# Two-stage transformer kernel on one core: mask rows sent two tiles earlier, a V copy and a table load moved at the turn of a row, and the next layer's weights loaded in the last row of a layer

## The reference, cut to what matters

```python
# first stage, per batch: 16 heads of 8, 256 queries, 1601 keys
scores = einsum('bhqd,bhkd->bhqk', qh, kh) / sqrt(8); scores = where(mask, -1e9, scores)
x1 = x + tanh(g_xattn) * (softmax(scores) @ vh @ w_o + b_o)
# second stage, six layers: 16 heads of 64, windows of 32 tokens and the window before
qkv = shift_tokens(x) @ Wqkv;  q, k = l2norm(q) * qs, l2norm(k) * ksc;  rotary(q), rotary(k)
x = x + softmax(8 * q k^T + local_mask) v @ Wo
xn = layernorm(shift_tokens(x)) ;  a, gate = split(xn @ W1 + b1)
x = x + (a * gelu(gate)) @ W2 + b2
out = x1 + tanh(g_ffn) * x
```

## Time and profile before

| | us |
|---|---|
| median of 3 runs (lowest, highest) | 5991.94 (5977.54, 5996.71) |
| the profiled execution: time, span | 6002.82, 6001.0 |
| PE busy | 5562.2 (93%) |
| ACT busy | 4052.7 (68%) |
| DVE busy | 3590.1 (60%) |
| POOL busy | 2654.8 (44%) |
| PE matmuls / POOL instructions | 51848 / 2280 |

### The profile page before, as it was taken

The page is one execution under the profiler, slowest core; times in us unless marked ns, Lnnn a source line. Parts: engine busy times, 40 slices in busy tenths (PEclk is TensorE's granted clock), DMA queues, the critical chain, the costliest instruction groups (busy, mean ns, idle before and its releaser), DMA issues.

```text
span 6001.0 us, 161497 instructions
## 1 busy us (share of the span) xinstructions
PE 5562.2 (93%) x51848; PEld 3310.2 (55%) x51848; DVE 3590.1 (60%) x7913; ACT 4052.7 (68%) x10886; POOL 2654.8 (44%) x2280
## 2 busy tenths in 40 slices
PE   5999999999999879999999999999998999999997
PEld 2444444444444356666666666666665666656665
DVE  3666666666666546655666566656665566556654
ACT  2555554555545467887878777877787778877885
POOL 2111221112211055655555555655565555655563
PEclk9999999999999989999999999999999999999998
DMA  3333233333334043233323333333333323333332
GB/s 79 68 73 62 56 69 64 74 59 58 67 65 74 14 134 98 89 95 108 100 92 92 102 104 94 92 96 108 94 92 97 106 94 92 93 111 93 92 93 74
DMA packets 146300, 512.29 MB, mean 85 GB/s; under 512 B 31996, under 2 KB 48252, under 8 KB 127404
## 3 DMA queue, kind: packets, MB, share of 16 engines
q1 hardware_dynamic: 144300, 506.02, 32.2%
q10 hardware_dynamic: 1536, 0.40, 0.0%
HBM read 223.41 MB, written 30.68 MB: 42 GB/s over the span
## 4 chain that ended last, share of the span: by engine, by line
PE 47%; ACT 9%; issue 4%; DVE 2%; DMA 1%; ACTq 0%; SPq 0%; POOL 0%; DVEq 0%; POOLq 0%
PE b_qk L1420 9%; PE b_c L1461 6%; PE b_o L1382 6%; PE b_pt L1363 5%; PE b_sc L1351 4%; PE b_nv L1398 3%; PE b_qk L1431 3%; PE b_nv L1451 2%; ACT probs L1131 2%; PE b_sc L1342 2%; PE b_c L1491 2%; ACT L78 1%; PE b_nv L1491 1%; ACT L1170 1%; DMA v<-v 1%
## 5 line engine op out<-in xcount | busy, mean ns | idle before, releaser
L441 ACT ACTIVATE eT<-b_e 128x512 f32<-128x512 f32 (+1 forms) x1664 | 907.6, 594 | 972.1 <-PE b_e L759 966.5
L1131 ACT ACTIVATE probs<-b_sc,nb,rq 128x96 f32<-128x96 f32 (+1 forms) x3072 | 1322.4, 449 | 41.1 <-DVE nb L1265 41.1
L514 DVE CUSTOM_DVE_ANT_0 junk<-b_s,mq 128x1024 bf16<-128x1024 f32 (+1 forms) x1024 | 1000.3, 991 | 436.8 <-PE b_s L741 412.2
L1062 POOL TENSOR_TENSOR probs<-probs,rsums 128x512 f32<-128x512 f32 (+1 forms) x768 | 716.4, 933 | 752.1 <-DVE rsums L1201 745.3
L1256 DVE TENSOR_REDUCE b_sc<-b_sc 128x4 f32<-128x512 f32 (+1 forms) x768 | 486.3, 633 | 878.0 <-PE b_sc L1351 877.7
L1121 ACT ACTIVATE probsT<-b_pt 128x512 f32<-128x512 f32 x768 | 457.5, 596 | 601.0 <-PE b_pt L1363 596.7
L1420 PE MATMUL b_qk<-xs,weights 128*128 128x256 f32 x3072 | 751.3, 389 | 87.7 <-POOL xs L1054 49.1
L755 PE MATMUL b_e<-mk,identb 128*128 128x512 bf16 (+1 forms) x1664 | 656.2, 394 | 54.2 <-DMA q_op<-mp 44.2
L1382 PEld LDWEIGHTS b_o<-probsT,v 128*64 128x64 f32 x9216 | 376.8, 138 | 572.6 <-issue 502.2
L1420 PEld LDWEIGHTS b_qk<-xs,weights 128*128 128x128 f32 x3072 | 562.8, 193 | 177.0 <-issue 64.5
L759 PE MATMUL b_e<-q_op,k_op 75*128 75x256 bf16 (+1 forms) x3328 | 659.3, 280 | 0.0
(11 more groups left out here) (132 smaller groups left out, 8344.9 us busy)
## 6 DMA issues: line engine op xcount, KB each, us to landing
rot_p<-rot_s SPq DMA_DIRECT2D x768, 256.0 KB, 2.4
rkb<-rk_scr SPq DMA_DIRECT2D x192, 512.0 KB, 5.9
k_op<-k_scr SPq DMA_DIRECT2D x576, 100.1 KB
v<-v SPq DMA_DIRECT2D x192, 256.0 KB, 3.6
k_scr<-kp SPq DMA_DIRECT2D x48, 400.2 KB, 3.5
ctxT<-in_ctx SPq DMA_DIRECT2D x17, 800.5 KB, 20.2
weights<-in_ffn_w SPq DMA_DIRECT2D x24, 512.0 KB, 5.3
q_op<-q_scr SPq DMA_DIRECT2D x144, 64.0 KB
```

Source lines behind the costliest of these rows:

```text
L441: nc.scalar.activation(eT[0:n, g % 2, i * 512:(i + 1) * 512], b_e[i][0:n, :], ACT.Exp).then_inc(s["e_ready"], 1)
L514: nc.vector.tensor_tensor_reduce(junk[:, half, 0:n], b_s[u % 2][:, 0:n], mq[:, p, qt, half * 1024:half * 1024 + n], 1.0, LOWEST, ALU.add, ...
L1062: nc.gpsimd.tensor_tensor(pu, pu, rsums[:, u % 2, :].unsqueeze(2).to_broadcast([P, 4, w]), ALU.mult).then_inc(s["pn_ready"], 1)
L1131: last = nc.scalar.activation(probs[:, t, k % 2, 2 * e + h, c0:P], b_sc[:, 512 * e + h * w:512 * e + (h + 1) * w], ACT.Exp, bias=nb[:, k % ...
```

## The change

It has three parts.

1. First stage: `TURN` is 5 instead of 7, and the three DMAs of the mask rows stand at tile `TURN + 3` = 8 instead of 10. The K projections move to tiles 3, 4, 6 and 7, the split of K on ACT by one tile (8 and 11), and POOL makes the mask rows of group 0 ahead of the first subtraction for K instead of behind it.
2. Second stage, turn of a row: the copy of the fourth V piece goes from ACT to DVE, behind the gate copies, with a semaphore of its own (`v3_kept`), and the exp and ln tables are loaded behind the first `probsT` of the next iteration instead of ahead of it.
3. Second stage, layers: the last two iterations of a layer stand outside the inner loop (five trips are left), and in the last one SP loads the next layer's scales, K, Q and V weights as soon as the last product that reads each has run; POOL makes the next layer's tables in its step 7. After layer 6 a further, unused set of weights (zeros) is loaded.

```diff
-TURN = 7
+TURN = 5
...
-                at += [(0, 3, "k", 0), (0, 4, "k", 1), (0, 5, "k", 2), (0, 6, "k", 3), (0, 9, "mean_q", 0),
-                       (0, 11, "var_q", 0), (1, 1, "q", 0), (1, 3, "v", 0), (1, 5, "v", 1), (1, 9, "v", 2),
+                at += [(0, 3, "k", 0), (0, 4, "k", 1), (0, 6, "k", 2), (0, 7, "k", 3), (0, 9, "mean_q", 0),
+                       (0, 11, "var_q", 0), (1, 1, "q", 0), (1, 3, "v", 0), (1, 7, "v", 1), (1, 9, "v", 2),
...
-                        if nxt and at == (0, 7):
+                        if nxt and at == (0, 8):
...
-                        if nxt and at == (0, 10):
+                        if nxt and at == (0, 11):
...
-                        if kt == 10:
+                        if kt == TURN + 3:
...
-                with hinted_loop(nc, eng, 1, NB // 2 - 1) as i:
+                with hinted_loop(nc, eng, 1, NB // 2 - 2) as i:
...
+                b = NB - 4
+                iteration(row(layer, b + 2, 0), row(layer, b + 1, 1), row(layer, b, 0), row(layer, b - 1, 1))
+                iteration(row(layer, b + 3, 1), row(layer, b + 2, 0), row(layer, b + 1, 1), row(layer, b, 0), LAST)
...
-                if not isinstance(layer, int):
-                    last = layer * NB - 1
-                    wait_apart(sp, sp_passed, s["qk_done"], count("qk_done", last, 8))
-                    load_scales(layer)
-                    load(PART_K, layer)
-                    load(PART_Q, layer)
-                    wait_apart(sp, sp_passed, s["v_done"], count("v_done", last, 4))
-                    load(PART_V, layer)
...
+                        if i == 1 and begin == LAST:
+                            load_scales(layer + 1)
+                            wait_apart(sp, sp_passed, s["qk_done"], count("qk_done", n, 4))
+                            load(PART_K, layer + 1)
...
+                    if begin == LAST:
+                        wait_apart(sp, sp_passed, s["qk_done"], count("qk_done", n, 8))
+                        load(PART_Q, layer + 1)
...
+                    if begin == LAST:
+                        wait_apart(sp, sp_passed, s["v_done"], count("v_done", n, 4))
+                        load(PART_V, layer + 1)
...
+                    if begin == LAST and k == 7:
+                        pool.wait_ge(scales_in, 16 * here[0] + 32)
+                        wait_apart(pool, pool_passed, s["rotc_ready"], count("rotc_ready", A[0], 8))
+                        scale_tables()
...
+                    if D and k == 0:
+
+                        load_tables(nc, act, EXP_LN_TABLES)
...
-                    if A and k >= 4:
+                    if A and 4 <= k < 7:
...
-                    load_tables(nc, act, EXP_LN_TABLES)
...
+                    if A and k == 7:
+                        n, _, p, _ = A
+                        dve.wait_ge(s["v_done"], count("v_done", n, 4))
+
+                        dve.wait_ge(s["o_done"], count("o_done", n, UNITS, back=2))
+                        nc.vector.tensor_copy(v[:, p, 1, 512:1024], b_qk[:, 512:1024]).then_inc(s["v3_kept"], 1)
```

More of the change, by code:

```diff
@@ L44 @@
 AHEAD = 2
+LAST = 3
 HX, DK = 16, 8
@@ L374, in iteration @@
                 for q in range(4):
[L375 to L379, removed]
                     if nxt and q == 1:
@@ L390, in iteration @@
                         max_parts(row, q)
+                    if nxt and q == 0:
+                        b = nxt[0]
+                        pool.wait_ge(s["khi_ready"], count("khi_ready", b, 1))
+                        nc.gpsimd.tensor_tensor(kf[:, :], kf[:, :], kp[:, 0, :], ALU.subtract
+                                                ).then_inc(s["kres_ready"], 1)
                     if nxt and q == 0:
@@ L829, in ffn_phase @@
                    norm_done=2, ln_ready=2, rn_ready=2, rnk_ready=1, rk_out=32, rkb_in=32, rqt_done=1, rq_ready=2,
-                   sum_ready=4, kn_ready=2, v_done=4, v_kept=4, vmid_in=32,
+                   sum_ready=4, kn_ready=2, v_done=4, v_kept=3, v3_kept=1, vmid_in=32,
                    scores_done=8, max_ready=8, nb_ready=8, exp_ready=8, rsum_ready=8, pn_ready=8,
@@ L837, in ffn_phase @@
                      rk_out="sp", rkb_in="sp", vmid_in="sp", rqt_done="pe", rq_ready="dve", sum_ready="pool", kn_ready="pool",
-                     v_done="pe", v_kept="act", scores_done="pe", max_ready="dve", nb_ready="dve", exp_ready="act",
+                     v_done="pe", v_kept="act", v3_kept="dve", scores_done="pe", max_ready="dve", nb_ready="dve", exp_ready="act",
                      rsum_ready="dve", pn_ready="pool", pt_done="pe", pt_kept="act", o_done="pe",
@@ L988, in iteration @@
                     n, _, p, _ = A
-                    wait_apart(sp, sp_passed, s["v_kept"], count("v_kept", n, 4))
+                    wait_apart(sp, sp_passed, s["v_kept"], count("v_kept", n, 3))
+                    wait_apart(sp, sp_passed, s["v3_kept"], count("v3_kept", n, 1))
                     wait_apart(sp, sp_passed, s["o_done"], count("o_done", n, UNITS, back=2))
@@ L1000, in _ @@
             sp.dma_start(out, xT[:, :, :]).then_inc(out_sent, 16)
+            sp.wait_ge(scales_in, 16 * DEPTH + 16)
+            for part in (PART_K, PART_Q, PART_V):
+                sp.wait_ge(part_in[part], 16 * DEPTH + 16)
             sp.wait_ge(out_sent, 16)
@@ L1015, in _, with scale_tables @@
             pool.wait_ge(consts_in, 16 * N_CONSTS)
+            here = [None]
             def layer_start(layer):
-                pool.wait_ge(scales_in, 16 * layer + 16)
-                wait_apart(pool, pool_passed, s["rotc_ready"], count("rotc_ready", layer * NB, 0))
+                here[0] = layer
+                if isinstance(layer, int):
+                    pool.wait_ge(scales_in, 16)
+                    scale_tables()
+            def scale_tables():
                 for i, col in enumerate((P_Q, P_Q, P_K, P_K)):
@@ L1368, in values @@
                     t, j0 = u // 4, 2 * (u % 4)
-                    pe.wait_ge(s["v_kept"], count("v_kept", n, 4))
+                    pe.wait_ge(s["v_kept"], count("v_kept", n, 3))
+                    pe.wait_ge(s["v3_kept"], count("v3_kept", n, 1))
                     if t == 1:
@@ L1414, in iteration @@
                             if i < 2:
-                                pe.wait_ge(s["v_kept"], count("v_kept", n, 3 + i, back=1))
+                                if i == 0:
+                                    pe.wait_ge(s["v_kept"], count("v_kept", n, 3, back=1))
+                                else:
+                                    pe.wait_ge(s["v3_kept"], count("v3_kept", n, 1, back=1))
                             else:
@@ L1634 @@
                           L0_xattn_b_k, L0_xattn_w_v, L0_xattn_b_v, L0_xattn_w_o, L0_xattn_b_o)
[L1635 to L1636 removed]
+    arrays.update(ffn_w=one_more(layer_weights(L0_ffn_Wqkv, L0_ffn_Wo, L0_ffn_W1, L0_ffn_W2)),
+                  ffn_vec=one_more(layer_vectors(L0_ffn_q_scale, L0_ffn_k_scale, L0_ffn_ln_g, L0_ffn_ln_b, L0_ffn_b1,
+                                                 L0_ffn_b2)),
                   rot=rotary_tables(), lmask=local_constants(),
```

3 lines of the change are left out of this document (1 added, 2 removed).

## The result

The changed kernel takes 5919.1 us (median of 4 runs, 5908.2 to 5932.1), the kernel before 5993.8 (4 runs) on the same chip: the ratio is 0.9883, with an interval of 0.9868 to 0.9899. It is 75 us faster by the medians and 70 by the ratio; 160 were forecast, and the time lies above the range. The profiled execution has a span of 5930.3 against 6001.0.

The account below looks back on a forecast made before the run. It took PE's work, its standstills and a lowered clock as the bound. Savings of 50 (first stage), 92 (turn of a row) and 18 (layers), 160 us, took the median 5991.9 to 5832; range 5770 to 5895.

Parts of the forecast that it names:

- First stage: -50 forecast: First stage: shorter mask-row waits and less half clock, minus a new `q_op` wait, save 50 us, between 0 and 95.
- the last of that part: First stage: moved K projections, POOL order and ACT split of K add no instruction and were costed at nothing.
- the mask rows' wait: First stage, PE before the transposed scores: of 44.2 us, 22 go at q = 3 and about 10 at q = 2.
- The new wait for `q_op`: First stage, near tile 5 of q = 2: PE waits 1 us a batch for `q_op`, 15 us in all.
- The granted clock: First stage: PE's granted clock was to rise from 0.96 to 0.98.
- the price of half clock: First stage: each us at half clock was priced at 0.47 us lost, some 66 us in the stage.
- the very term of the forecast: First stage: half of the 66 us lost to half clock goes with the waits, 33 us saved.
- Turn of a row: -92 forecast: Second stage: PE no longer waits before `b_o`; each of 92 rows gains 1.0 us, bounds 30 to 135 in all.
- Both limits: Second stage, turn of a row: `hT` and the exponentials limit the gain to 1.0 us, not the wait's 1.47.
- Layers: -18 forecast: Second stage, layer tops: four gain 3 us each, the first 7, layer 6's last row loses 1; between 0 and 40.
- The straight-line iterations cost nothing: Second stage: iterations moved outside the inner loop cost 0, as rows 39.07 us apart, some already straight, showed no stall.
- the first stage gives nothing: Rival, chance 0.20: the first-stage standstill moves from tile 0 to tile 5 of q = 2; 5882 us, up to 5905.

Follow-up runs that it names:

- kres_small: Changed kernel with POOL's first-stage subtraction for K cut to 16 columns, the rest of the residue left out; ratio 0.9821 to the kernel before.
- cross_only: Kernel before with only the first-stage part of the change; ratio 1.0047 to the kernel before, 28 us slower.
- q_first: Changed kernel with SP's stores of Q and `q_op` loads put ahead of the `k_op` loads of group 0; ratio 0.9923 to the kernel before.
- best: Changed kernel with DVE's `mneg` before reciprocals, `y` after tile 9's maxima, POOL's `mq` after q = 1's maxima, no inner layer loop; ratio 0.9744 to the kernel before.
- mq_late: Changed kernel with POOL's product `mq` moved behind the maxima of q = 1, a group later; ratio 0.9843 to the kernel before.
- turn_only: Kernel before with only the V copy on DVE and the later table load; ratio 0.9853 to the kernel before, 88 us faster.
- copy_only: Kernel before with only the V copy moved to DVE, the second table load staying ahead of `probsT`; ratio 0.9909 to the kernel before, 55 us faster.
- layers_only: Kernel before with only the shortened inner loop and the early weight loads and tables; ratio 1.0006 to the kernel before.
- ffn_only: Changed kernel with its first-stage part taken back; ratio 0.9856 to the kernel before.
- straight: Changed kernel without the inner loop of a layer, all sixteen iterations straight code; ratio 0.9897 to the kernel before.
- turn6: Changed kernel with TURN 6 instead of 5 and K projections at tiles 3, 4, 5 and 7; ratio 0.9910 to the kernel before.

## Why the prediction was right and wrong

**First stage: -50 forecast, +24 in the trace (+16 and +28 by the ratios).** The step that failed is the last of that part: "The moved K projections, the POOL order and the ACT split of K add no instruction; PE shows no standstill at them and the K chain is used a group later, so I cost them at nothing." They do add no instruction. But they put POOL's subtraction and `mq` later, onto `y` and `xq`, and with `TURN` at 5 they put a K projection behind `mneg`, with a reciprocal of 1.74 us and a product of 0.65 ahead of it on DVE. That was 24.2 us (the fall of the `smax` wait in `kres_small`), 16.4 and 19.0, some 60 us of PE's time that my sum had at nothing. Taken away one by one they gave 30, 25 and 27 us, clock and all; taken away together the stage is 44 us shorter than before, near the 50.

The other terms of this part held. Of the mask rows' wait the forecast had all 22 us ahead of q = 3 go, and 10 of those ahead of q = 2: by group it fell from 19.9 to 2.9 and from 24.3 to 15.3. In `cross_only` it fell to 2.6 and, for q = 2, not at all (25.7). Ahead of q = 2 the DMAs stayed behind the `k_op` loads, which `q_first` showed. The new wait for `q_op` came at the place named, 13.0 us by the list where I had 15. Some of that is luck: the 10.1 us by which I placed it are those of the store `q_scr<-qp`, and the landing of the loads that PE waits for stands in no row.

The granted clock rose from 0.96 to 0.97, not 0.98. Why it rose isn't shown: PE waited 98.5 us in the five rows above, where it was 52.3 before, and with the same first stage `cross_only` has 0.96. By the price of half clock 0.01 is worth 16 us here, so more waits and the better clock make 46 - 16 = 30 us, near the 24. `best` has the term whole: its four waits are 58.3 us in all (8.8 of it one wait in the last batch), about the 52.3 of the kernel before, and yet the stage is 44 us shorter; by the price (0.47, from one stretch of one batch) its 0.98 in place of 0.96 is worth 0.02 x 2 x 1745 x 0.47 = 33 us, the very term of the forecast, as far as a clock printed to two places can tell. That the clock falls less there because the waits are short ones is argued, not shown.

That `y` and `xq` are slow because of POOL's instructions beside them is shown twice, from both sides: `kres_small` freed one, `mq_late` the other. The Trainium skill, "SBUF — State Buffer", section "SBUF: two separate sides", has the rule: DVE and GpSimd share one port pair, which a DVE instruction with two inputs in SBUF and a GpSimd instruction that reads SBUF hold as an exclusive lock, so that the later one waits for the whole of the other. By that rule `y` and `xq` would end shortly behind POOL, and they do, 0.26 to 0.29 us behind. I hadn't asked it of an edit that shifts POOL's work by one tile.

**Turn of a row: -92 forecast, -82 in the trace of `turn_only`, -88 by its ratio.** Right in each step and off in size: 38.28 us between rows for the 38.07 forecast, 0.8 a row for 1.0. Both limits were named, and both bind by a few tenths (0.20 and 0.36). `copy_only` splits it: removing the copy from ACT alone gives 0.50, near the copy's 0.62. No drain of the table load appears, as the forecast held against the Trainium skill, "ScalarE: Activation LUTs", section "What ACT_TABLE_LOAD costs": the load ends at 3524.97 and the exponential starts at 3524.99.

**Layers: -18 forecast, nothing in `layers_only`, 8 to 14 less in the changed kernel by the Gelus.** The trace of the changed kernel gives 14.4 (96.0 - 81.6), but some of that is luck of the one trace: by the median of seven with its second stage, 3674.5, it is 8.4, and by the ratios `ffn_only` and `turn_only` are equal. Most of it is the first layer, from its first Gelu to the next layer's: 616.1 us for the 624.5 of `turn_only`, where the forecast had 7 for a top with no branch backwards. The four middle layers, where it had 3 each, gained 2.0 us in all (2498.7 to 2496.7), and in `ffn_only` they lost 0.8.

Their tops gained what was said: 89.3 us for two rows, 86.3 with the turn alone, 82.6 in the changed kernel. The step that failed is "The straight-line iterations cost nothing". The iterations cost next to nothing; leaving the loop doesn't. Before, the exit of the inner loop stood at the end of the layer, next to the top with its 3.34 us. Now it stands two rows ahead, as a stall of its own, 2.08 us on PE and 2.11 on DVE, with the top's 3.76 still there. The two rows at the exit are 81.8 us where 76.6 would be undisturbed, more than the 3.7 that the top gains. That the exit is the cause is shown by `straight`: without it the four middle layers take 2485.0 us, 13.7 less than in `turn_only` or 3.4 each, for the 3 of the forecast. That both stalls are late instructions is an inference from "issue" in the rows; nothing here measured a fetch.

The probabilities had "the first stage gives nothing" at 0.20, with 5882 to 5905. It was that case and a little worse, though not for the reason written there: the wait at tile 5 was in the sum already.

## What to carry to other kernels

An edit that adds no instruction can still cost: for each instruction that it moves, list what then runs beside it on the other engines, DVE and POOL above all, and whether both read SBUF. Here a DVE instruction with two SBUF operands was late by whatever POOL had left to do, and the margins that had kept them apart were as small as 0.07 and 0.26 us, which no view calls a wait. The sign of it is the mean duration of one line, compared between two traces. When a loop is shortened to make room for a special last trip, its exit moves too, and here it cost 5.2 us where the top gained 3.7; make the whole stretch straight, or put the exit where PE stands anyway. And take more than one trace before a few microseconds of a stage are put down to an edit: the same code differed by 27 us in the first stage and by 11 in the second.

## What the runs showed of the hardware

- A DVE addition or product of 128 x 256 floats with both operands in SBUF takes 0.42 us, and in the changed kernel 2.0 to 2.7 beside a POOL instruction of 2.9 to 3.2 us; it ends 0.26 to 0.29 us behind it, in 29 of 29 cases. It was slow in every kernel with the overlap, and where one of the two overlaps was taken away, that one was fast.
- The one that starts first isn't held up. In `turn6` one `xq` starts at 140.13, 0.06 us ahead of POOL's `mq`: `xq` takes 0.41 us, and `mq` 3.08 for the 2.86 it takes elsewhere.
- Leaving a loop of hinted branches costs PE 1.8 to 2.4 us at five of the changed kernel's six exits and DVE 2.1 to 2.2 at all six, in which they wait for nothing that the profile shows. In `layers_only` DVE's part is 4.6 to 5.7.
- The order of three groups of DMAs on one engine's queue only moved the wait: 31.2 us for mask rows and `q_op` became 40.5 for `k_op`.
